# Cross attention of all heads: norms moved from VectorE to ScalarE, context rows loaded a stage sooner

## The reference

```python
x = _layernorm(x + _L0_attn_ref(x, ...))      # a recurrence with an inner gradient step
x = _layernorm(x + _L0_xattn_ref(x, ctx, ctx, bias, ...))   # cross attention, one head
x = _layernorm(x + _L0_ffn_ref(x, ...))       # 8 experts, the 2 best of each token
x = _layernorm(x + _L1_attn_ref(x, ...))      # causal, 16 heads
x = _layernorm(x + _L1_xattn_ref(x, ctx, ctx, mask, ...))   # cross attention, 16 heads
x = _layernorm(x + _L1_ffn_ref(x, ...))
```

```python
qp, kp = _proj(q, W1, b1, W2, b2), _proj(k, W1, b1, W2, b2)
qk = einsum('bqd,bkd->bqk', qp, kp) / sqrt(256) + mask
return einsum('bqk,bkd->bqd', softmax(qk), v1)
```

## Time and profile before

| | us |
|---|---|
| median of 3 runs | 1983.69 (1982.69 to 1984.71) |
| the profiled execution | 1984.26 |
| its span in the trace | 1982.2 |
| busy PE, DVE, ACT, POOL in the span | 1784.5, 1424.2, 1056.6, 680.9 |

### The profile page before, as it was taken

How to read it: one execution, slowest core, us unless ns; L and a number is a source line. 1 busy time by engine, 2 the same in 40 slices (tenths; PEclk the granted TensorE clock), 3 DMA queues, 4 the chain that set the end, 5 groups by cost and what they waited for, 6 DMA issues and landing times. The chain is left out here.

```text
span 1982.2 us, 33777 instructions
## 1 busy us (share of the span) xinstructions
PE 1784.5 (90%) x13052; PEld 1000.6 (50%) x13052; DVE 1424.2 (72%) x2385; ACT 1056.6 (53%) x1706; POOL 680.9 (34%) x779
## 2 busy tenths in 40 slices
PE   8998888959999999888999899779999999999786
PEld 4787556747888888642333365312222222223364
DVE  1523588755777777677777378899999999995663
ACT  1221444515555555344666533248888888787542
POOL 0654775013444444341332024403341212111442
PEclk9999899969999999996999999869999999999998
DMA  5132877555666666260111157502210101000000
GB/s 188 49 110 99 299 267 268 186 204 217 258 258 256 257 255 252 79 205 16 30 34 27 44 176 213 168 11 78 82 35 18 35 18 34 18 18 1 25 12 32
DMA packets 108275, 239.32 MB, mean 121 GB/s; under 512 B 28378, under 2 KB 79102, under 8 KB 104640
## 3 DMA queue, kind: packets, MB, share of 16 engines
q1 hardware_dynamic: 81156, 198.12, 28.5%
q0 software_dynamic: 24848, 36.95, 6.9%
q10 hardware_dynamic: 2112, 2.10, 0.3%
HBM read 180.78 MB, written 55.74 MB: 119 GB/s over the span
## 5 line engine op out<-in xcount | busy, mean ns | idle before, releaser
L1938 DVE TENSOR_REDUCE Eh_maxima<-Eh_max 128x2 f32<-128x802 f32 x512 | 474.9, 988 | 21.2 <-PE Eh_max L1817 16.4
L1926 ACT ACTIVATE Eh_probs<-Eh_pair 128x1024 f32<-128x1024 f32 (+1 forms) x288 | 287.5, 998 | 118.1 <-PE Eh_pair L1856 118.1
L1300 PE MATMUL C_y<-C_x_high,C_W 128*128 128x256 f16 x1472 | 250.2, 274 | 1.5 <-DVE C_x_low L1538 1.5
L1817 PE MATMUL Eh_max<-Eh_KS,Eh_QS 49*128 49x401 f16 x1024 | 198.7, 358 | 49.7 <-DVE Eh_maxima L1938 39.4
L1879 PE MATMUL Eh_av_ps<-Eh_probs,E_V 128*17 128x512 f32 (+1 forms) x1664 | 223.9, 611 | 0.0
L1300 PE MATMUL C_y<-C_x_low,C_W 128*128 128x256 f16 x736 | 201.5, 274 | 0.0
L1938 DVE TENSOR_REDUCE Dh_maxima<-Dh_max 128x2 f32<-128x1024 f32 x128 | 152.1, 1222 | 44.2 <-PE Dh_max L1825 42.1
L1926 ACT ACTIVATE Eh_probs<-Eh_single 128x512 f32<-128x512 f32 x272 | 161.7, 595 | 29.5 <-PE Eh_single L1856 29.4
L1817 PEld LDWEIGHTS Eh_max<-Eh_KS,Eh_QS 49*128 49x128 f16 x1024 | 50.7, 94 | 238.5 <-DVE Eh_maxima L1938 198.4
L1655 POOL DMA_DIRECT2D Eh_KS<-E_kd x64 | 37.1, 579 | 357.7 <-PE Eh_pair L1856 352.0
L1300 PEld LDWEIGHTS C_y<-C_x_high,C_W 128*128 128x128 f16 x1472 | 144.3, 98 | 18.8 <-issue 1.7
(11 more groups left out here) (398 smaller groups left out, 3641.5 us busy)
## 6 DMA issues: line engine op xcount, KB each, us to landing
C_W<-w_split SPq DMA_DIRECT2D x23, 3072.0 KB, 11.5
w_split<-B_w_parts SPq DMA_DIRECT2D x24, 768.0 KB, 4.6
B_places<-in_w_experts_dram SPq DMA_DIRECT2D x18, 768.0 KB, 7.0
Eh_KS<-E_kd POOLq DMA_DIRECT2D x64, 150.1 KB, 3.3
C_tail<-in_expert_tail_dram SPq DMA_DIRECT2D x23, 384.0 KB, 8.0
A_QT<-in_w_experts_dram SPq DMA_DIRECT2D x8, 768.0 KB, 5.2
w_split<-A_QT SPq DMA_DIRECT2D x8, 768.0 KB, 6.8
early_ctxT<-in_ctxT_dram SPq DMA_DIRECT2D x6, 800.5 KB, 6.7
```

The lines of the kernel that those rows point to most:

```text
L1300: last = mm(y_ps[n % Y_BANKS][:, i, :], W[:, u, a, at_w:at_w + P], x[:, s % 2, k, :], start=(q == 0), stop=(q == len(parts) - 1))
L1817: last = self.nc.tensor.matmul(bank[:, a, 0:self.cw], self.QS[r, slot, p, qt * P:(qt + 1) * P], self.KS[r, slot, p, k0:k0 + self.cw], star ...
L1926: self.nc.scalar.activation(dst, src, ACT.Exp, scale=1.0 / SCORE).then_inc(self.exp_done, 1)
L1938: self.nc.vector.tensor_reduce(self.maxima[:, g % 2, :, p * TPB + qt, c], self.max_ps[n % 2][:, :, 0:self.cw], AX_X, ALU.max).then_inc(sel ...
```

## The change

1. **Context rows sooner.** `early.more`, two new slots that belong to both stages, takes the two large N pieces of batch 0. SyncE loads them in the recurrence, once its inversion is over, behind the seventh store. The recurrence's buffers G64, CT and P1 now lie in the same memory. In the next stage slots 2 and 3 are these; SyncE's loads begin with the small N piece, biases and weights in turn, the router's after them.
2. **Who splits.** ScalarE and VectorE split the third N piece of batch 0 too, both before the first maximum; GpSimd only the second.
3. **Deviations ahead of the last piece.** In the recurrence GpSimd takes batch 0's before the last piece and batch 1's before its third operation.
4. **Norms by ScalarE.** For batches 0 to 2 of the cross attention GpSimd also computes shift = -mean x deviation (`shift_of`, two small operations), and ScalarE computes X x deviation + shift behind its share of the queries. VectorE keeps the last batch.
5. **Last batch.** Its statistics are taken tile by tile, three tiles are normed before the last result is added and transposed at once, only the fourth is left for after it. Two dummy matmuls (`spin`) stand between the transposes, one at the recurrence's end. The second copy into XT is VectorE's.

The diff, cut to its core:

```diff
+    def inverse_deviation(self, pool, c, tiles=None):
+
+        first, end = tiles or (c * TPB, (c + 1) * TPB)
+        g = slice(first, end)
+        pool.wait_ge(self.mv_ready, end)
         self.nc.gpsimd.tensor_scalar(self.var_eps[:, g], self.mv[:, g, 1], self.eps, 1.0,
                                      ALU.add, ALU.mult).then_inc(self.ve_ready, 1)
         pool.wait_ge(self.ve_ready, c + 1)
         self.nc.gpsimd.tensor_tensor(self.rstd[:, g], self.var_eps[:, g], self.neg_half[:, g],
                                      ALU.pow).then_inc(self.rstd_ready, 1)
...
+    def shift_of(self, pool, c, shift, shift_ready):
+
+        g = slice(c * TPB, (c + 1) * TPB)
+        self.nc.gpsimd.tensor_scalar(shift[:, g], self.mv[:, g, 0], -1.0, 0.0, ALU.mult, ALU.add).then_inc(shift_ready, 1)
+        pool.wait_ge(shift_ready, 2 * c + 1)
+        pool.wait_ge(self.rstd_ready, c + 1)
+        self.nc.gpsimd.tensor_tensor(shift[:, g], shift[:, g], self.rstd[:, g], ALU.mult).then_inc(shift_ready, 1)
...
+    early_flat = early.more[:].rearrange("p s w -> p (s w)")
+    G64, CT, P1 = (early_flat[:, i * 4 * TPB * HB:(i + 1) * 4 * TPB * HB].rearrange("p (b c) -> p b c", b=4) for i in range(3))
...
             for c in range(B - 2, B):
                 turn_group(nc, pe, X, ident[:], banks[6:8], c, norm.normed, copied, turned)
+            spin(nc, banks[2][:], ident[:], XT[:, 0, 0:S], 1)
...
             for i in range(len(PIECES_AT), 3 * SPLIT_FROM):
+                last = i - 3 * (SPLIT_FROM - 1)
+                if last in (0, 2):
+                    norm.inverse_deviation(pool, last // 2)
                 early.piece(pool, *divmod(i, 3))
                 if i == len(PIECES_AT) + 2:
                     early.scale_bias(pool)
-            for c in range(B):
+            for c in range(2, B):
...
+        sp.wait_ge(steps_done, steps)
+        for i in range(2):
+            k0, k1 = N_PIECES[i]
+            sp.dma_start(self.more[:, i, 0:(k1 - k0) * D].rearrange("p (k d) -> p k d", d=D),
+                         self.dram["ctx"][0, k0 * P:k1 * P].rearrange("(k p) d -> p k d", p=P)).then_inc(self.more_loaded[i], 16)
...
-        return job[0] != "W" and job != ("N", 0, 0)
+        return job[0] != "W" and job not in (("N", 0, 0), ("N", 0, 2))
...
+        return early.ctxT[:, s, :] if s < 2 else early.more[:, s - 2, :] if s < 4 else places[:, s - 4, :]
...
-            for j in range(2, len(jobs) + RING_SLOTS):
+            for j in range(4, len(jobs) + RING_SLOTS):
                 if j >= RING_SLOTS + 2:
                     wait_split(sp, j - RING_SLOTS)
                     if jobs[j - RING_SLOTS][0] == "W":
                         store(j - RING_SLOTS)
                 if j < len(jobs):
                     load(j)
-                if j == 4:
+                if j < 4 + TPB - 1:
+                    t = j - 3
+                    sp.dma_start(bias[:, t - 1, :], dram["fside"][t * P:(t + 1) * P]).then_inc(bias_loaded[t], 16)
+                if j == 4 + TPB - 1:
                     route.sync(sp)
-                    for t in range(1, TPB):
...
-            turn_x(B - 1)
+
+            def turn_last(h, tiles):
+                r = use[("x", B - 1, h)]
+                for t in tiles:
+                    last = nc.tensor.transpose(ring[r % 3][:, t * P:(t + 1) * P], X[:, (B - 1) * TPB + t, h * P:(h + 1) * P], ident[:])
+                return last
+
+            pe.wait_ge(norm.normed, NT - 1)
+            for h in range(KD):
+                ring_free(use[("x", B - 1, h)])
+                turn_last(h, range(TPB - 1))
+            spin(nc, scores_ps[:, 0:S], ident[:], XT[:, 0, 0:S], 2)
+            pe.wait_ge(norm.normed, NT)
+            for h in range(KD):
+                turn_last(h, [TPB - 1]).then_inc(ring_ready, 1)
...
+            def normalize(c):
+                act.wait_ge(shift_ready, 2 * (c + 1))
+                for t in range(c * TPB, (c + 1) * TPB):
+                    a(X[:, t, :], X[:, t, :], ACT.Identity, bias=shift[:, t:t + 1], scale=norm.rstd[:, t:t + 1]).then_inc(norm.normed, 1)
...
+            split_high(pieces.index[("N", 0, 2)])
...
+                if t == NORM_AT and b >= 1:
+                    normalize(b - 1)
...
             norm.setup(pool)
             split(("N", 0, 1))
-            scale_bias(1)
-            split(("N", 0, 2))
-            for t in range(2, TPB):
+            for t in range(1, TPB):
                 scale_bias(t)
             for b in range(B):
                 if b + 1 < B:
                     split(("T", b + 1, 0))
                 if b >= 1:
                     norm.inverse_deviation(pool, b - 1)
+                    norm.shift_of(pool, b - 1, shift, shift_ready)
                 if b + 1 < B:
                     split(("T", b + 1, 1))
                     for i in range(3):
                         split(("N", b + 1, i))
-            norm.inverse_deviation(pool, B - 1)
+            norm.inverse_deviation(pool, B - 1, (NT - TPB, NT - 1))
+            norm.inverse_deviation(pool, B, (NT - 1, NT))
...
+            split_low(pieces.index[("N", 0, 0)])
+            split_low(pieces.index[("N", 0, 2)])
             maximum(0)
-            split_low(pieces.index[("N", 0, 0)])
...
-                if t == NORM_AT and b >= 1:
-                    norm.normalize(dve, b - 1)
                 if t == QUERY_AT and b + 1 < B:
                     queries(b + 1)
                 if t == ROUTE_AT and b >= 1:
                     route.vector(dve, b - 1, route_ps(b - 1))
+                if n > NT - TPB:
+                    norm.statistics_of(dve, n - 1, sum_ready)
+            dve.wait_ge(norm.rstd_ready, B)
+            for t in range(NT - TPB, NT - 1):
+                norm.normalize_of(dve, t)
             add(NT - 1)
-            norm.statistics(dve, B - 1, sum_ready)
-            norm.normalize(dve, B - 1)
+            norm.statistics_of(dve, NT - 1, sum_ready)
+            dve.wait_ge(norm.rstd_ready, B + 1)
+            norm.normalize_of(dve, NT - 1)
+            r = use[("x", B - 1, KD - 1)]
+            dve.wait_ge(ring_ready, highs(r + 1))
+            v.tensor_copy(XT[:, KD - 1, (B - 1) * S:], ring[r % 3][:])
```

46 lines of the change are left out of this document (28 added, 18 removed).

## The result

| | before | after |
|---|---|---|
| median, us | 1984.2 (1982.69 to 1985.62) | 1951.83 (1948.34 to 1952.37) |
| ratio | | 0.9836, 95% interval 0.9811 to 0.9862 |
| the profiled execution, its span | 1984.26, 1982.2 | 1952.37, 1950.6 |

Forecast were 1951 us and a range of 1943 to 1962. The kernel is 1.6% faster. The table shows what the spans' difference of 31.7 us is made of. Its stretches go from the start of a stage, or of TensorE's transposes of a tile's probabilities, to the next. A boundary goes from the transposes of tile 6 or 10 to those of X behind them; the stretches between, 39.7 and 36.2 us, didn't change.

The account below looks back on a forecast made before the run. The prediction took engines waiting on each other in the first 419 us as the bound, TensorE's idle and slow time being recoverable; 7.0 + 4.9 + 18.4 - 0.3 + 3.0 = 33.0 us gave 1951, range 1943 to 1962.

Parts of the forecast that it names:

- Boundaries: Two cross-attention batch boundaries: ScalarE's norms remove the stall behind VectorE's normalisations, 18.4 us (17 to 18.7).
- at most 0.3 lost at each: At each of the two boundaries, TensorE's possible wait for VectorE's queries, done by 283.4: at most 0.3 us.
- Recurrence's end: End of the recurrence: earlier deviations remove TensorE's 4.44 us wait and the slow clock behind it, 7.0 us (4.0 to 7.2).
- may hold the cast back a little: Recurrence's end: two context loads (1.57 MB) issued behind the store the cast waits for may delay it; 7.0 taken, not 7.2.
- Start: Start of the cross attention: first attend begins 3.7 us sooner and loses 2.2 of slow clock, less 1.0: 4.9 us (1.5 to 7.4).
- The charge of 1.0: Behind the cross attention's start: GpSimd's next splits fall beside VectorE's weight splits, costing 1.0 us (0 to 2).
- I take 0: Start of the cross attention: later first maximum against clock kept by the dummy, net 0, between 2.4 us late and 1.5 won.
- Last batch: Cross attention's last norms: tile-by-tile statistics and two transposes instead of eight end it at 414.6, gaining 3.0 us (1.5 to 4.0).
- The first (contention in a new place): Rival: moved VectorE work meets GpSimd at the context pieces' low halves and recurrence's fourth normalisation, 7 us, 1958; chance 0.14.
- The second (a stall that remains): Rival: at the boundaries the queries' low halves stay behind a 4.45 us weight split, 2 x 4 us, 1959; chance 0.10.
- The third: Rival: at three boundaries ScalarE waits for GpSimd's shift, 21 us late each, making the kernel slower, 1988; chance 0.03.
- The fourth: Rival: another wait hides the recurrence's end and cross attention's start; only boundaries and end pay, 1963; chance 0.07.

Follow-up runs that it names:

- vector_quiet: Changed kernel with norms of batches 0 to 2 back on VectorE ahead of the queries' low halves, GpSimd held until they are done: 1952.5 us, ratio 0.9859.
- vector_behind: Changed kernel with norms of batches 0 to 2 back on VectorE, behind the queries' low halves, GpSimd working on: 1958.9 us, ratio 0.9891.
- alone_deviation: Kernel before the change with only GpSimd's deviations of batches 0 and 1 moved ahead of the last piece's first and third operation: 1975.7 us, ratio 0.9969.
- after_again: The changed kernel profiled and timed a second time, nothing altered: 1948.7 us, ratio 0.9836.
- undo_last: Changed kernel with the last batch of the cross attention normed as before the change, without its dummies: 1953.6 us, ratio 0.9854.
- undo_deviation: Changed kernel with GpSimd's deviations of batches 0 and 1 behind the last weight piece again: 1950.4 us, ratio 0.9841.

## Why the prediction was right, point by point

- **Boundaries, 18.4 forecast.** 18.6 in the comparison, 18.5 and 19.0 undone. The cause given (each normalisation held for an operation of GpSimd, the queries' low halves behind them, TensorE behind these) is shown by vector_quiet and, with the same engine in another place, by vector_behind. Only that each of the four waits for a whole operation isn't so: the first waits for what is left of one (1.56 us, beside the end of one of 2.86, in before). The "at most 0.3 lost at each" was 0.3 at the first and 0 at the second. ScalarE's norm, taken as 0.5, took 0.52; the third boundary cost 0.4 for 0.3.
- **Recurrence's end, 7.0.** 7.45 in the comparison and 7.6 in the trace of alone_deviation. But the wait that the working starts from isn't fixed: it was 4.4 us in both profiles of before, and with the other parts in place, in an execution in which GpSimd was early, the undoing brought 2.09 back and cost 2.3. What made GpSimd early is open. That the context loads "may hold the cast back a little" didn't show (it waited 0.58, before 0.50).
- **Start, 4.9.** 5.3 seen, 5.9 to 6.4 undone. "What ends last then is VectorE's rest" holds, at 208.07 against the attend's 208.21. The charge of 1.0 for GpSimd's splits beside weight splits lies within what was seen: tile 1 to 6 got 0.7 us shorter in the first profile and 0.5 longer in the second. "I take 0" for the clock of the first scores failed in form: they became fast, and the second ones slow in the first profile and not in the second, where 1.7 us more were won.
- **Last batch, 3.0.** 3.3 in the comparison, and the working holds: it took the slow attend of before, and the addition behind three normalisations that don't wait for the attend. Forecast was an addition 0.7 us behind its old time, which was 0.12 behind the attend's end; it came 0.60 behind a slow attend's end in after_again, and 2.24 behind the fast one in after, at the same distance from tile 15. With a fast attend in both kernels only 1.6 are left (undo_last), a condition that the forecast doesn't name. Mis-sized were the dummies, each counted as 0.46 at full clock: the two took 1.88 us and not 0.92, which fitted into the wait.
- **"From 420 us on no engine's work changes ... what the first two stages save the end saves."** The first half holds, the second doesn't: the stages behind scatter by 16 us with the clock. With the rest of before, the profiled execution would have been 1948.7; the sum of the parts was short by 2.4 us and the longer rest hid it.
- **Rivals.** The first (contention in a new place) was there with 0.35 us of the 7 it needed. The second (a stall that remains) fell: the weight split of 4.45 us was there at 264.29, and cost 0.3. The third fell: ScalarE begins its norms with no wait for the shift at any of the three boundaries. The fourth fell: both first terms paid, the first of them less than forecast in undo_deviation.

## What to carry to other kernels

When each of a row of short operations grows to the length of a neighbour's operation, what costs is the neighbour and not the load (7.90 us for four beside GpSimd, 1.37 without): look at what the other engine does in that moment, and either move the short ones to an engine that isn't held (ScalarE here) or let the neighbour wait; the two differ by about 1 us here, where 18.5 to 19.0 were at stake. A term read from one profile of one kernel holds where that kernel's other waits stand; undone from the other side it may be a third. What a new order gains can also depend on what it no longer waits for: the last batch gained 1.6 us beside a fast attend and 3.3 beside a slow one, and one comparison doesn't tell them apart. And where 1500 us of unchanged work behind a change scatter by 16 us, a gain under 5 is told by the stretch where it falls, not by the end time.

## What was not expected of the hardware

VectorE's 128x256 norms on SBUF are held up beside GpSimd (7.90 against 1.37 us for four), its 128x512 low halves that read PSUM aren't (1.39 beside GpSimd's cast at 275.89, 1.40 beside another in vector_quiet). By the Trainium skill (SBUF — State Buffer, Who interferes with whom) a VectorE instruction with one SBUF input outside its two-port modes doesn't contend with GpSimd, and a tensor_scalar in such a mode does: the low halves have one input in SBUF and one in PSUM, and the rows agree.

Four ScalarE norms whose single durations are 0.59 us take 2.07 together: each begins 0.49 us behind the one before and overlaps it by 0.1.

Behind 1.6 us of idle time TensorE's 24 matmuls took 5.71 to 5.92 us in three traces (granted clock 0.71 to 0.73 on average, so partly at 1.2 GHz) and 4.24 in a fourth, at 2.4 GHz. The attend of tile 15 took 4.42 us in four traces and 5.84 to 6.09 in ten, behind the same two waits of 0.57 and 0.30 us and the router's 16 small matmuls.
